# Cross-attention and spline FFN on one core: the down residual moved into a peeled first FFN, float32 products split into f32r products, a new order of stages

## The reference, cut to what matters

```python
query = teacher_features @ Wq.T + bq          # context, [512, 128]
key = teacher_features @ Wk.T + bk
attention = softmax(query @ key.T)            # [512, 512]
x = x + layernorm(x) @ attention.T            # mixes hidden columns
n = layernorm(x)
x = x + (silu(n @ gate_w.T) * (n @ up_w.T)) @ down_w.T
```

## Time and profile before

| what | value |
|---|---|
| median of 3 runs | 312.27 us (311.22 to 312.31) |
| profiled execution, its own time | 310.22 us |
| span of its trace | 308.4 us |
| mean granted clock | 0.945 of 2.4 GHz |
| busy: TensorE, VectorE, GpSimd, ScalarE | 279.8, 183.0, 162.5, 155.2 us |
| DMA | 25.25 MB, mean 82 GB/s |

### The profile page before, as it was taken

How to read it: one execution, slowest core, us unless ns; L and a number is a source line. 1 busy time by engine, 2 the same in 40 slices (tenths; PEclk the granted TensorE clock), 3 DMA queues, 4 the chain that set the end, 5 groups by cost and what they waited for, 6 DMA issues and landing times.

```text
span 308.4 us, 3946 instructions
## 1 busy us (share of the span) xinstructions
PE 279.8 (91%) x1232; PEld 200.8 (65%) x1232; DVE 183.0 (59%) x319; ACT 155.2 (50%) x261; POOL 162.5 (53%) x141
## 2 busy tenths in 40 slices
PE   0757499977999999999999999999999999899995
PEld 0322134756477788884777888947778889377894
DVE  0389885897645676663466766634667666443503
ACT  1424244223588891334888913348889133286710
POOL 4099546387656466214564662145646621398630
PEclk9998555895999999999999999999999999999999
DMA  7999436000070000011800000117000001100003
GB/s 203 254 402 384 180 92 251 0 0 0 0 307 36 2 1 2 0 68 68 339 1 0 0 0 0 68 68 272 0 0 0 0 0 68 70 0 1 2 0 136
DMA packets 6950, 25.25 MB, mean 82 GB/s; under 512 B 1308, under 2 KB 1820, under 8 KB 5084
## 3 DMA queue, kind: packets, MB, share of 16 engines
q1 hardware_dynamic: 6940, 25.13, 22.6%
HBM read 20.93 MB, written 4.19 MB: 81 GB/s over the span
## 4 chain that ended last, share of the span: by engine, by line
PE 77%; DVE 9%; DMA 5%; SPq 3%; ACT 2%; issue 2%; POOL 1%; DVEq 0%; ACTq 0%; POOLq 0%
PE bank L1242 10%; PE bank L1273 10%; PE bank L1244 10%; DMA coef<-in_g_coef 5%; PE bank L1259 5%; PE bank L1257 5%; PE bank L1256 5%; PE bank L1228 4%; PE bank L1180 4%; PE bank L1203 4%; PE bank L1202 4%; PE bank L1204 4%; PE bank L1119 3%; PE bank L1280 3%; PE bank L1161 3%; PE bank L1217 3%
## 5 line engine op out<-in xcount | busy, mean ns | idle before, releaser
L1076 POOL TENSOR_TENSOR il<-inter,ih 128x512 fp32r<-128x512 f32 x64 | 86.3, 1361 | 44.6 <-ACT ih L762 24.9
L928 DVE TENSOR_TENSOR inter<-inter,bank 128x512 f32<-128x512 f32 x64 | 43.7, 686 | 44.7 <-ACT inter L758 44.6
L758 ACT ACTIVATE inter<-bank 128x512 f32<-128x512 f32 x64 | 37.9, 596 | 16.2 <-PE bank L1244 13.6
L762 ACT ACTIVATE ih<-inter 128x512 fp32r<-128x512 f32 x64 | 39.3, 630 | 2.5 <-DVE inter L928 2.3
L733 ACT ACTIVATE qk<-bank,nmr,rstd 128x512 f32<-128x512 f32 x16 | 12.5, 780 | 43.4 <-PE bank L1204 26.0
L1273 PEld LDWEIGHTS bank<-d_r,ih 128*128 128x128 f32 x256 | 32.6, 191 | 1.8 <-ACT ih L762 0.7
L1273 PE MATMUL bank<-d_r,ih 128*128 128x256 f32 x256 | 33.4, 284 | 0.0
L1064 POOL TENSOR_TENSOR xres<-x,ones 128x2048 f32<-128x2048 f32 x4 | 14.4, 3600 | 27.7 <-DMA out<-xres 25.8
L1242 PE MATMUL bank<-xh,gate_r 128*128 128x512 f32 x64 | 27.0, 422 | 1.7 <-DVE zg L920 1.7
L1256 PE MATMUL bank<-ih,d_u 128*128 128x512 f32 x64 | 27.9, 436 | 0.0
L1202 PE MATMUL bank<-ph,xh 128*128 128x512 f32 x64 | 26.0, 407 | 0.0
(11 more groups left out here) (94 smaller groups left out, 524.5 us busy)
## 6 DMA issues: line engine op xcount, KB each, us to landing
x<-in_x SPq DMA_DIRECT2D x4, 1024.0 KB, 4.8
xT<-in_xT SPq DMA_DIRECT2D x4, 1024.0 KB, 6.9
out<-xres SPq DMA_DIRECT2D x16, 256.0 KB, 2.1
ctxT<-in_ctxT SPq DMA_DIRECT2D x4, 512.0 KB, 7.5
rd<-in_d_r SPq DMA_DIRECT2D x2, 1024.0 KB, 6.0
knots<-in_d_knot SPq DMA_DIRECT2D x1, 1280.0 KB, 13.8
d_pt<-in_d_node SPq DMA_DIRECT2D x1, 1024.0 KB, 19.7
d_coef<-in_d_coef SPq DMA_DIRECT2D x1, 1024.0 KB, 21.7
```

Source lines behind the costliest of these rows:

```text
L758: nc.scalar.activation(inter[:, m % 3], gbank[m % 2][:], ACT.Silu).then_inc(s["silu_done"], 1)
L762: nc.scalar.activation(ih[:, m], inter[:, m % 3], ACT.Copy).then_inc(s["ih_done"], 1)
L928: V.tensor_tensor(inter[:, m % 3], inter[:, m % 3], ubank[m % 2][:], ALU.mult).then_inc(s["mult_done"], 1)
L1076: G.tensor_tensor(il[:, m % 2], inter[:, m % 3], ih[:, m].bitcast(f32), ALU.subtract).then_inc(s["il_done"], 1)
```

## The change

1. The down residual leaves the preparation. `spread` and `residual` keep r = 0 to 7. New stages `down_spread(m)` and `down_residual(m)`, m = 0 to 15, make one tile of `d_r` each, through `zgbank`, a ring of four product tiles and one table `d_r` loaded in two halves. They stand in `ffn_first`, a copy of the FFN for batch 0 outside the loop, which now runs for b = 1 and 2.
2. The projection of all batches, and `qk` and the scores of batches 1 to 3, are three f32r products of high and low parts each in place of one float32 product. New splits: `split_weights` and `split_basis` once, `split_ctx(a)` per batch, the low part of `qk` on VectorE. `cast_t` on ScalarE writes `xn2r` direct from PSUM, and VectorE subtracts it to get `xn2l`. Batch 0 keeps float32 for `qk` and scores.
3. All three lists of stages and the list of loads are in a new order. The tables and tiles share memory in new ways, with waits for it.

TensorE's queue in the new `ffn`, with e for energy, db for down basis, pt for `prob_t`: `project`, `qk(a)`, gate_up 0 to 3, e0, 4, e1, db0, db1, 5, db2, 6, e2, db3, db4, 7, 8, db5, 9, 10, db6, e3, db7, 11, db8, 12, db9, pt0, 13, pt1, 14, pt2, db10, pt3, 15, db11, `down` 0 (13 tiles), db12, db13, `xm` 0, rest of `down` 0, `xm` 1 to 3, `down` 1, db14, db15, `down` 2, two `norm_t`, `down` 3, `norm_t`, tail 0, `norm_t`, tails 1 to 3. ScalarE's: `ctx`, `zg`, two copies of `qk`, Silu 0, 1, `ih` 0, Silu 2, `ih` 1, Silu 3, `ih` 2, Silu 4, `ih` 3, Exp 0, `ih` 4, Exp 1, Silu 5, 6, `ih` 5, 6, Silu 7, 8, `ih` 7, Silu 9, `ih` 8, Silu 10, `ih` 9, Exp 2, 3, Silu 11, `ih` 10, Silu 12, `ph` 0, Silu 13, `ih` 11, `ph` 1, `ih` 12, `ph` 2, `ih` 13, Silu 14, `ph` 3, `xh`, Silu 15.

The new `attention_only` begins with the powers, `qk(0)`, the scores and softmax, then the windows; the eight gate residuals stand from `split_basis` to the end, `down_nodes` before them and `jumps` last.

The stages of the down residual in `ffn_first`, and the core of the rest:

```diff
@@ -331,238 +335,378 @@
+        def ffn_first(st, b, a):
+
+            st.project(b)
+            st.down_residual(0)
+            st.down_spread(0)
+            st.gate_up(b, 0)
+            st.down_residual(1)
+            for m in range(1, 3):
+                st.down_spread(m)
+            st.gate_up(b, 1)
+            st.activate(b, 0)
+            st.down_spread(3)
+            st.round_inter(b, 0)
+            st.gate_up(b, 2)
+            st.down_spread(4)
+            st.down_residual(2)
+            st.gate_up(b, 3)
+            st.down_residual(3)
+            st.activate(b, 1)
+            st.down_residual(4)
+            st.split_ctx(a)
+            st.activate(b, 2)
+            st.round_inter(b, 1)
+            st.down_basis(b, 0)
+            st.down_residual(5)
+            st.round_inter(b, 2)
+            st.activate(b, 3)
+            st.down_residual(6)
+            st.down_spread(5)
+            st.qk(a)
+            st.activate(b, 4)
+            st.down_spread(6)
+            st.gate_up(b, 4)
+            st.down_basis(b, 1)
...
         def program(eng, st):
             attention_only(st)
-            with eng.Fori(0, B - 1) as b:
+            ffn_first(st, 0, 1)
+            with eng.Fori(1, B - 1) as b:
                 ffn(st, b, b + 1)
             ffn(st, B - 1)
...
@@ -577,35 +721,38 @@
...
+            load(spread[:].rearrange("p m n -> p (m n)"), "d_spread", "spread_in")
+
+            sp.wait_ge(s["energy_mm"], NT)
+            load(g_basis.rearrange("p a n -> p (a n)"), "g_basis", "basis_in")
+            half = d["d_r"].rearrange("p (h n) -> h p n", h=2)
+            sp.wait_ge(s["xm_mm"], NT)
+            sp.dma_start(rd_a[:].rearrange("p m k n -> p (m k n)"), half[0]).then_inc(s["rda_in"], 16)
+            sp.wait_ge(s["pT_mm"], NT)
+            sp.dma_start(rd_b[:].rearrange("p m k n -> p (m k n)"), half[1]).then_inc(s["rdb_in"], 16)
...
@@ -651,9 +798,28 @@
...
+                        dst = qk if first(b) else qk_h
+                        nc.scalar.activation(dst[:, n], abank[n][:], ACT.Identity, bias=bqk[:, n:n + 1]).then_inc(s["qk_done"], 1)
+
+                def split_ctx(b):
+                    act.wait_ge(s["ctx_in"], 16 * (b + 1))
+                    act.wait_ge(s["xm_mm"], NT * b)
+                    nc.scalar.activation(ctx_h, ctxT[:], ACT.Copy).then_inc(s["ctx_hi"], 1)
...
@@ -735,7 +907,7 @@
...
-                    nc.scalar.activation(xn2T[:, t], abank[t % 2][:], ACT.Copy).then_inc(s["xn2t_copied"], 1)
+                    nc.scalar.activation(xn2r[:, t], abank[t % 2][:], ACT.Copy).then_inc(s["xn2r_done"], 1)
...
@@ -793,7 +966,25 @@
...
+                    if first(b):
+                        return
+                    dve.wait_ge(s["out_mm"], NT * (b - 1))
+                    for n in range(2):
+                        dve.wait_ge(s["bqk_in"], 2 * 16)
+                        dve.wait_ge(s["qk_done"], 2 * b + n + 1)
+                        V.scalar_tensor_tensor(qk_l[:, n], abank[n][:], bqk[:, n:n + 1], qk_h[:, n].bitcast(f32), ALU.add, ALU.subtract).then_inc(s["qkl_done"], 1)
+
+                def split_ctx(b):
+                    dve.wait_ge(s["ctx_hi"], b)
+                    V.tensor_tensor(ctx_l, ctxT[:], ctx_h.bitcast(f32), ALU.subtract).then_inc(s["ctx_split"], 1)
...
@@ -833,21 +1024,39 @@
...
+                def down_residual(m):
+                    dve.wait_ge(s["dres_mm"], m + 1)
+                    dve.wait_ge(s[("rda_in", "rdb_in")[m // (MT // 2)]], 16)
+                    if m == 0:
+                        dve.wait_ge(s["zg_mm"], 1)
+                    if m >= RING:
+                        dve.wait_ge(s["dres_done"], m - RING + 1)
+                    part = (rd_a, rd_b)[m // (MT // 2)][:, m % (MT // 2)].rearrange("p k n -> p (k n)")
+                    V.tensor_tensor(prod_d[:, m % RING].rearrange("p k n -> p (k n)"), zgbank[:], part, ALU.mult).then_inc(s["dres_mul"], 1)
...
-                    V.tensor_copy(xn2r[:, t], xn2T[:, t]).then_inc(s["xn2r_done"], 1)
+                    dve.wait_ge(s["xn2r_done"], NT * b + t + 1)
+                    V.tensor_tensor(xn2l[:, t], abank[t % 2][:], xn2r[:, t].bitcast(f32), ALU.subtract).then_inc(s["xn2l_done"], 1)
...
@@ -990,13 +1208,19 @@
...
+                def down_residual(m):
+                    pool.wait_ge(s["dres_mul"], m + 1)
+                    if m == 0:
+                        pool.wait_ge(s["node_mm"], 2 * CLS)
+                        pool.wait_ge(s["res_mm"], GATE_RES)
+                        pool.wait_ge(s["du_done"], CLS)
+                    G.tensor_tensor(d_r[:, m], prod_d[:, m % RING, 0], prod_d[:, m % RING, 1], ALU.add).then_inc(s["dres_done"], 1)
...
@@ -1101,22 +1326,51 @@
...
+                    if first(b):
+                        pe.wait_ge(s["ctx_in"], 16)
+                    else:
+                        pe.wait_ge(s["ctx_split"], b)
+                        pe.wait_ge(s["wqk_split"], 1)
+                        pe.wait_ge(s["xn2l_done"], NT * b)
                     for n in range(2):
                         for c in range(CTX // P):
-                            last = mm(abank[n][:], wqk[:, n, c], ctxT[:, c], start=c == 0, stop=c == CTX // P - 1)
+                            start, stop = c == 0, c == CTX // P - 1
+                            if first(b):
+                                last = mm(abank[n][:], wqk[:, n, c], ctxT[:, c], start=start, stop=stop)
+                            else:
+                                mm(abank[n][:], wqk_h[:, n, c], ctx_h[:, c], start=start, stop=False)
+                                mm(abank[n][:], wqk_l[:, n, c], ctx_h[:, c], start=False, stop=False)
+                                last = mm(abank[n][:], wqk_h[:, n, c], ctx_l[:, c], start=False, stop=stop)
                         last.then_inc(s["qk_mm"], 1)
...
+                        mm(abank[t % 2][:], qk_h[:, 0, c], qk_h[:, 1], start=True, stop=False)
+                        mm(abank[t % 2][:], qk_l[:, 0, c], qk_h[:, 1], start=False, stop=False)
+                        last = mm(abank[t % 2][:], qk_h[:, 0, c], qk_l[:, 1], start=False, stop=True)
...
@@ -1138,18 +1392,23 @@
...
+                def down_spread(m):
+                    if m == 0:
+                        pe.wait_ge(s["zg_done"], 1)
+                        pe.wait_ge(s["spread_in"], 16)
                         pe.wait_ge(s["jump_split"], 2)
+                    pe.wait_ge(s["dres_mul"], m)
                     for k in range(2):
-                        dst = bank[2 * (r % 2) + k]
-                        if r < 2 * CLS:
-                            c = slice(r % CLS * HID, (r % CLS + 1) * HID)
-                            last = mm(dst[:], pick[:, r // CLS, r % CLS, k], win_hl[:, c], start=True, stop=True)
-                        else:
-                            for n in range(2):
-                                m = 2 * (r - 2 * CLS) + n
-                                last = mm(dst[:, n * STRIP:(n + 1) * STRIP], spread_[:, m], in_blocks(jump[k], m // CLS), start=True, stop=True)
-                    last.then_inc(s["res_mm"], 1)
+                        last = mm(zgbank[:, k * STRIP:(k + 1) * STRIP], spread_[:, m], in_blocks(jump[k], m // CLS), start=True, stop=True)
+                    last.then_inc(s["dres_mm"], 1)
...
@@ -1221,11 +1480,14 @@
...
                     for a in range(CLS):
-                        last = mm(zgbank[0:G_K, :], g_basis[:, a], xn2T[:, a], start=a == 0, stop=a == CLS - 1)
+                        pe.wait_ge(s["xn2l_done"], NT * b + a + 1)
+                        mm(zgbank[0:G_K, :], g_basis_h[:, a], xn2r[:, a], start=a == 0, stop=False)
+                        mm(zgbank[0:G_K, :], g_basis_l[:, a], xn2r[:, a], start=False, stop=False)
+                        last = mm(zgbank[0:G_K, :], g_basis_h[:, a], xn2l[:, a], start=False, stop=a == CLS - 1)
```

606 lines of the change are left out of this document (377 added, 229 removed).

## The result

The changed kernel takes 313.96 us (median of 12 runs, 312.62 to 315.48), the kernel before 311.56 beside it (12 runs, 309.44 to 312.82): ratio 1.0084 [1.0055, 1.0114]. The forecast was 309.0 and faster. The time lies in the range (299 to 317), which was wide enough for either sign; the forecast's sign was wrong.

The account below looks back on a forecast made before the run. VectorE's queue was taken to bound the preparation, TensorE's the FFNs. Preparation -11.5, first FFN +7.8, second and third together +1.8, last -1.4 sum to -3.3: 309.0 us against the median of 312.27, range 299 to 317.

Parts of the forecast that it names:

- the walk of VectorE's queue: Preparation: new order followed queue by queue, putting the first gate product at 72.5 instead of 84.0, -11.5 us.
- rival 3: Preparation: gains only 5 us because its half-clock waits stay; 315.5 us in all, chance 0.10.
- second count: Preparation: old chain minus removed work plus added work puts the first gate product at 74.9.
- pair of spreads: First FFN: spreads 1 and 2 stand together, so TensorE waits a whole round, 0.85 us.
- saving of 2.1: Second and third FFN: three f32r products replacing each float32 product save 2.1 us per FFN.
- (a): Second and third FFN: Silu's table load behind qk's copies delays tile 2's up product 1.4 us, against 0.2 before.
- (b): Second and third FFN: softmax cut in two adds two table loads; TensorE waits 0.9 us before the probability transpose.
- (c): Second and third FFN: the split of xT ends 0.8 us after TensorE reaches the first xm.
- rival 4: ScalarE: a mid-work table switch costs twice its 1.28 us; 314.1 us in all, chance 0.05 together with rival 5.
- Rival 1: FFNs: new order as tight as the old, most forecast stalls vanish; 301.5 us in all, chance 0.27.
- Rival 2: First FFN: the spreads' single bank makes most spreads wait up to 0.85 us each; 319 with twelve, chance 0.13.
- rival 5: Projection, qk, scores: three split products cost one float32 product, losing 6.3 us; 315.3, chance 0.05 together with rival 4.

Follow-up runs that it names:

- e11: e9 with jump inputs back behind the node products, GpSimd's powers behind the first window split, one spread behind a gate product; 0.9826 of the kernel before.
- e2: Changed kernel plus ten unread filler products on TensorE in the preparation; 1.0035 of the kernel before.
- e8: e7 without its filler products; 1.0154 of the kernel before.
- e7: Changed kernel with old FFN order, GpSimd's d_v products waiting for xT's split, jumps behind the projection, first gate product before first spread, fillers; 0.9971 of the kernel before.
- e10: Changed kernel with old orders of preparation, later FFNs and loads, the down residual still out of the preparation; 1.0306 of the kernel before.
- e1: Changed kernel with projection, qk and scores as single float32 products again, low parts made but unused; 1.0265 of the kernel before.
- e4: Changed kernel with the old FFN order for batches 1 to 3, context split at its head; 0.9964 of the kernel before.
- e9: e7 with the jumps split around the projection, their GpSimd inputs earlier, first two gate products interleaved with spreads; 0.9965 of the kernel before.
- e12: e11 plus filler products behind the projection and before the third and fifth spreads; 0.9794 of the kernel before.
- e3: Changed kernel with GpSimd's four d_v products waiting until VectorE has split xT; 1.0037 of the kernel before.

## Why the prediction was wrong

**Failed step: the preparation, -11.5 for -5.2, in the walk of VectorE's queue.** This is rival 3, at 0.10. The walk had the first gate residual at 42 and the first gate product 30.5 later; they came at 45.4 and 33.4 later. So 3.4 of the missing 6.3 us lie before the first gate residual and 2.9 behind it.

The first part is mostly VectorE beside GpSimd: the walk took 0.62 for each split, and I never set GpSimd's queue beside VectorE's to see which operations meet. With GpSimd set apart (e11) the first gate residual comes 28.4 us behind M where the changed kernel has 30.7: 2.3 us. The rest is about the late start of this execution (M 14.7, where the ten other kernels with the new order have a median of 13.1).

In the second part the walk had one queue, VectorE's, with 3 us of waits. They are 4.8, for copies of node products at half clock above all, and the operations take 1.1 more than 42 x 0.63. Half clock makes a second chain of nearly the same length: node products, transposes, and a projection of 4.8 us where it takes 3.2 at 2.4 GHz, which the working did not price at half clock at all. In the changed kernel the jumps leave VectorE at 76.9, and ScalarE has its copy of the projection from 77.2 on:

```profile
75.60 1.35 DVE L1097 TENSOR_TENSOR wqk<-win,wqk 64x512 bf16<-64x512 f32 x2
77.80 0.75 DVE L1129 SCALAR_TENSOR_TENSOR zg<-zg,g_low,bank 102x512 fp32r<-102x512 f32 x1 [0.84 <-ACT zg L921]
```

e2, e8 and e7 show that either chain alone holds the gate product. One reading misled here: the 21.5 of 27.3 us at half clock are those from 28.7 to 56, and not the chain's end from 57.6 on, where VectorE was busy 22.1 of 26.4 us at a mean clock of 0.87. That the half clock would stand at the very end (0.59 there) was not asked. My second count (74.9) and its upper bound of 79 knew of half-clock waits; I took the walk because it kept the order of waits, and weighed its optimism too low.

**What the removed work was worth.** The prediction's second count read the preparation's gain as work taken off VectorE. e10 speaks against it: with the work gone and the old places kept, G is at 87.7, and even without the collision of 3.3 no earlier than before. The gain needed the new order; whether that order would have gained as much with the work still there was not run.

**First FFN, +7.8 for +9.3.** The work was priced well: TensorE is busy for 61.5 where the sum had 61.0 without stalls. Stalls were put at 1.8 and are 2.8. The pair of spreads cost 0.8 as said. Missed was 1.4 before the third score product, whose bank waits for an Exp. ScalarE and VectorE of the changed kernel there:

```profile
105.89 1.28 ACT L835 ACT_TABLE_LOAD   x1 [1.50 <-DVE prod_d L1042]
107.18 0.69 ACT L835 ACTIVATE prob<-bank,nmax 128x512 f32<-128x512 f32 x1
```
```profile
105.10 0.68 DVE L1042 TENSOR_TENSOR prod_d<-bank,rd_b 128x512 f32<-128x512 f32 x1
```

`prob` lies in the memory of the down residual's buffers, so its first Exp waits for the last product of sixteen; my walk followed engines and banks, and left out who shares memory.

**Second and third FFN, +0.9 each for +0.8 and +0.5.** Right in sum by luck, two errors against each other. The saving of 2.1 is 1.3 to 1.4 by e1, and the new order costs 0.5 more busy time than e4. The stall (a) of 1.4 isn't there. ScalarE in the second FFN:

```profile
149.04 0.69 ACT L803 ACTIVATE qk_h<-bank,bqk 128x512 fp32r<-128x512 f32 x1 [0.71 <-PE bank L1343]
149.75 0.60 ACT L930 ACTIVATE inter<-bank 128x512 f32<-128x512 f32 x1
```

No table load stands between the last copy and the first Silu: Silu's table is still in from the FFN before. I had carried over the load ahead of the first Silu without asking what had displaced that table: a load at 138.93, at the head of the loop's body, which the second FFN of the changed kernel does not have. (b) and (c) are there, 0.8 and 0.7 named for 0.9 and 0.8. That ScalarE goes to Exp and back to Silu twice in an FFN instead of once (four loads, not the five forecast) costs no drain either:

```profile
170.24 0.20 ACT L835 ACTIVATION_READ_ACCUMULATOR prob<-bank,nmax 128x1 f32 x1
170.45 1.28 ACT L930 ACT_TABLE_LOAD   x1
171.75 0.60 ACT L930 ACTIVATE inter<-bank 128x512 f32<-128x512 f32 x1
```

From the end of one to the start of the next function 1.31 us pass, as in the earlier trace rows; rival 4 falls. The drain of about 1.38 that the Trainium skill gives (ScalarE: Activation LUTs, "What ACT_TABLE_LOAD costs") is not seen in this kernel.

**Last FFN and rivals.** -1.4 for -1.1. Rival 1, that the new order is as tight as the old, did not hold: the new order gave 1.5 to 1.7 us per FFN away (e4). Rival 2 fell with the spreads' waits, rival 5 with e1. Had I compared the two orders by stalls alone, against 61.72 of 61.77, a new order could only lose.

**What stays open.** The rows of e1 put the split's saving at 1.8 of the 2.1; where the last 0.4 or so goes is not known. The new preparation's order was not changed step by step: 4.5 of its 11.4 us are there at the first maximum and 3.3 are the collision in e10, the other 3.6 have no experiment of their own.

## What to carry to other kernels

When a stage has idle engines on every side, write down every chain of nearly its length before pricing one: here a queue of VectorE and TensorE at half clock were equally long, and taking one away alone brought the next stage forward by 0.2 or 1.1 of the 5.9 us that both gave. Then count to the end of the next stage, since work that was only moved comes back there. Before work goes into a hole of GpSimd, look at what VectorE reads at that time; ahead of a stretch that TensorE fills, a few idle products in the waits can be worth more than the waits. An FFN order in which TensorE already never waits is to be kept when only the products in it get cheaper.

## What the runs showed of the hardware that I had not expected

VectorE and GpSimd hold each other up when both read from SBUF. A VectorE operation with two SBUF operands takes 0.69 alone and 1.67 beside GpSimd's addition (e11, e9), a window split 0.74 and 1.75, GpSimd's addition 1.28 and up to 2.27. With an operand in PSUM nothing changes (0.68). The wait can be long: in e10 a normalisation that takes 0.52 otherwise took 3.81 and ended 0.3 us behind GpSimd's copy of 3.60. The Trainium skill, SBUF — State Buffer, section "SBUF: two separate sides", describes the port pair of the two as an exclusive lock, taken for a whole instruction by an operation with two SBUF inputs; the rows agree in size, since an addition of 0.69 that waits for a part or all of GpSimd's 1.28 comes to between 0.69 and 1.97, and 1.67 lies there.

TensorE's granted clock fell to 1.2 GHz behind or within waits that look harmless: in e2 behind 3.2 us without products, in e7 within one of 2.4, in e11 behind 1.8 and 0.3. Each time it stayed down for 7 to 10 us, in which a product takes 0.43 instead of 0.23 from start to start; with the waits filled (e12) it stayed up in the profiled execution. The waits alone do not decide it. In e9, with 1.7, 0.3 and twice 0.8, it stayed up, and of two executions with the same waits of 1.5 and 0.8, e3 lost it for 3.4 us and the changed kernel did not. The same kernels had other mean clocks in other runs. What else decides is not shown here. In e11 the spans of six runs differ by 3.4 us, which is more than most of what this study was about.
